# A gated cross-attention block with a routed feed-forward layer: shorter operand stacks, extra TensorE sums, two batches routed together

## The chip, the cores and the metric

One core of one Trainium2 chip runs the whole program. The metric is the device time of one execution in microseconds (us). A tick is the kernel's own unit of order: in one tick each engine handles a fixed list of 16 slots.

## The reference

For 8 batches of 256 tokens with 128 features, and 64 context rows per batch:

```
x = x + tanh(g_xattn) * (attention(layernorm(x), ctx) @ Wout + bout)   # 16 heads of 8; keys: 64 context rows, then the tokens, causal
x = x + tanh(g_ffn) * moe(layernorm(x))
moe:  logits = xt @ Wg + bg; two best of 8 experts per token
      seq = cumsum(one_hot, axis=0)          # a token's place in its expert; over 320 it is dropped
      h = silu(disp @ W1) * (disp @ W2); out = h @ W3      # 320 places per expert, hidden 512
      y = sum over the two experts of softmax weight * out[place]
```

## The kernel before, in words

**First part (0 to 36 us).** Tokens are normalised, turned by TensorE (PE) and multiplied with the query, key and value weights, batch by batch. Queries and keys are needed at fp32 accuracy from bf16 multiplies, so each is split into three bf16 parts (`qp`, `kp`): ScalarE (ACT) writes part 0 and, from a difference that VectorE (DVE) forms (`parts`), part 1; GpSimd (POOL) writes part 2 (`third_parts`). 

**Stacks.** Transfers then pile six pairs of parts on top of one another: for each head of a pair (`par`), `load_q` and `load_k` write six times 8 rows into `qst` and `kst` (48 rows, `QROW`), so that one matmul of 48 rows adds all six products. The stack has 64 rows (`KROWS`): the remaining 16 are -1 in two rows and 0 elsewhere in `kst`, and 0 in `qst`, written by transfers from `fill` and `zeros` (L384, L389). Two of these rows of `qst` are later overwritten with the row maxima (`load_maxima`, L407), so that the second matmul of the scores subtracts the maximum by itself. Batches are loaded in groups of 1, 1, 2, 2, 2. SyncE (SP) issues most transfers, in this order: the parts of group 0, the first halves of group 1, the large fixed-row transfers of groups 1 to 4, a quarter of group 2, then, tick by tick, the maxima of a unit followed by a further quarter of a group. ACT issues the other halves of group 1 (`load_quarter(act, 1, 1)`, `load_quarter(act, 1, 3)`, twelve transfers) before it enters its tick loop, whose first work is the copy of the first unit's maxima (`maxima_row`, L665).

**Units and ticks.** A unit is four head pairs of one batch; there are 16. Unit U is scored in tick U-2 (`scores`: queries on the partitions, only for the maxima, L1037 to L1053), its maxima are reduced by DVE (`maxima`), split and turned (`maxima_t`, L1102) and copied (`maxima_row`) and sent into the stack in tick U-1, it is scored again in tick U with keys on the partitions (`scores_t`, L1070) and exponentiated (`exponentials`, L672), and multiplied with the values in tick U+1 (`values`, L1087), whose result is turned and normalised in tick U+2. A batch is then projected, added to x, normalised, turned, given its logits (`logits`) and routed: `top_two` and `destinations` on DVE, `positions` on PE (places by a triangular matmul, L1165), and four indirect transfers on POOL (`send_rows`, L576). The order on every engine is written out by the constants `AT_...`: a batch's `top_two` begins in tick 3 after its second unit, slot 12; `positions` is in tick 4, slot 13; the rows are sent in tick 5, slots 4, 6, 12 and 20. POOL, DVE, PE and ACT all run their slots in that order, so a wait holds up all that stands behind it on its engine.

**Experts.** When all rows have landed in `slots_dram`, SP loads each expert's 320 rows (`ex`), PE turns them (`turn`, L1207) and runs three matrix multiplies per expert (L1217, L1219, L1230), ACT applies silu, DVE multiplies, and POOL adds the rows to the output with indirect transfers (L607).

PE's code waits, ahead of its first tick, for all constants and for the last difference of the split:

```python
            pe.wait_ge(consts, N_CONSTS)
            pe.wait_ge(cast, 1)
            pe.wait_ge(rq_done, B)
            pe.wait_ge(rk_done, B)
```

## Time and profile before

| | us |
|---|---|
| median of 3 runs (313.08 to 314.41) | 314.01 |
| the profiled execution, its own time | 315.55 |
| its span in the trace | 313.4 |
| PE / DVE / POOL / ACT busy | 220.9 / 174.9 / 153.4 / 131.0 |

"Busy" counts the time an engine has an instruction in work. Rows give start and duration in us from the span's start; `<-` in brackets names what ended an engine's idle time. The granted clock of PE is a share of 2.4 GHz: 1.0 is 2.4 GHz, 0.5 is 1.2 GHz. `ACTq` and `SPq` are the issuing side of those engines, where a transfer is handed to the queue.

### The profile page before, as it was taken

What the parts mean: (1) busy time and instruction counts of PE and PEld (TensorE: products, weight loads), DVE (VectorE), ACT (ScalarE), POOL (GpSimd) and SP (SyncE); (2) the same over time, 40 slices, a digit from 0 to 9 for tenths busy, and PEclk for the clock granted to TensorE, in tenths of its full rate; (3) what the DMA queues carried; (4) which work ended last, traced back from release to release, by engine and by line L of the source; (5) the groups of instructions that cost most, each with busy time, mean ns of one, the idle gap of its engine ahead of it and who ended that gap; (6) DMA issues with size and microseconds to landing.
All of it is one profiled execution on the core that took longest, in us unless ns stands there. A gap on an engine that the chain in (4) does not pass through costs nothing.

```text
span 313.4 us, 6289 instructions
## 1 busy us (share of the span) xinstructions
PE 220.9 (70%) x2308; PEld 138.4 (44%) x2308; DVE 174.9 (56%) x556; ACT 131.0 (42%) x294; POOL 153.4 (49%) x208
## 2 busy tenths in 40 slices
PE   1878360068898777878888878784049999999830
PEld 0656220044554444444444434343027777777630
DVE  6666390047988998989898962434203333333310
ACT  6479400055766656656565665311023222222200
POOL 6698800014445457382736555453700554654662
PEclk9999755556999999999999985755558999999995
DMA  6342799545354333556110010001045345555220
GB/s 193 76 85 57 92 101 131 123 118 103 98 107 67 51 53 69 85 105 204 32 47 11 18 42 12 3 14 35 9 106 134 83 107 113 119 110 119 23 21 5
DMA packets 30237, 24.14 MB, mean 77 GB/s; under 512 B 4041, under 2 KB 27011, under 8 KB 30208
## 3 DMA queue, kind: packets, MB, share of 16 engines
q1 hardware_dynamic: 23104, 18.08, 28.2%
q0 software_dynamic: 4608, 4.16, 7.6%
q10 hardware_dynamic: 2496, 1.52, 1.8%
q8 instruction: 18, 0.29, 0.4%
q14 instruction: 11, 0.09, 0.1%
HBM read 9.27 MB, written 5.82 MB: 48 GB/s over the span
## 4 chain that ended last, share of the span: by engine, by line
PE 48%; DVE 14%; POOL 10%; issue 8%; ACTq 8%; ACT 7%; DMA 2%; POOLq 1%; SPq 0%; DVEq 0%
PE PS L1087 11%; PE PS L1230 8%; PE PS L1217 7%; ACTq L330 6%; PE PS L1219 6%; PE PS L1070 5%; DVE mx L794 3%; ACT pt L672 3%; PE PS L1137 2%; DVE mx L793 2%; POOL slots L576 2%; ACTq L338 2%; POOL rstd L566 2%; PE PS L1154 1%; PE PS L1040 1%
## 5 line engine op out<-in xcount | busy, mean ns | idle before, releaser
L672 ACT ACTIVATE pt<-PS 128x512 f32<-128x512 f32 x128 | 69.3, 593 | 40.9 <-PE PS L1070 40.7
L607 POOL DMA_INDIRECT out<-kst x24 | 36.4, 1518 | 43.9 <-DVE kst L972 31.1
L793 DVE TENSOR_REDUCE mx<-PS 128x2 f32<-128x384 f32 x64 | 35.4, 552 | 34.3 <-PE PS L1053 33.7
L794 DVE TENSOR_REDUCE mx<-PS 128x2 f32<-128x640 f32 x64 | 52.0, 812 | 0.0
L1087 PE MATMUL PS<-pt,vp 128*32 128x256 f32 (+2 forms) x768 | 48.2, 348 | 4.8 <-POOL pt L558 4.8
L1070 PE MATMUL PS<-qst,kst 64*128 64x256 bf16 (+2 forms) x384 | 27.6, 254 | 28.0 <-DMA qst<-mrow 18.2
L555 POOL TENSOR_SCALAR_AFFINE_SELECT pt<-pt 128x512 f32<-128x512 f32 x32 | 21.5, 672 | 52.7 <-ACT pt L672 52.6
L576 POOL DMA_INDIRECT slots<-rows,dest x32 | 32.2, 1005 | 14.6 <-issue 7.6
L963 DVE TENSOR_TENSOR kst<-PS,kst 128x320 f32<-128x320 f32 x32 | 15.7, 491 | 38.5 <-ACT kst L730 38.5
L1070 PEld LDWEIGHTS PS<-qst,kst 64*128 64x128 bf16 x384 | 14.9, 98 | 47.2 <-issue 20.2
L730 ACT ACTIVATE kst<-PS 128x320 f32<-128x320 f32 x32 | 14.0, 438 | 46.7 <-PE PS L1219 46.7
L1217 PE MATMUL PS<-kst,kp 128*128 128x320 f32 x64 | 25.3, 478 | 0.6 <-ACT kst L719 0.6
L1230 PE MATMUL PS<-kp,kst 128*128 128x128 f32 (+1 forms) x192 | 24.3, 279 | 1.3 <-issue 1.1
L1230 PEld LDWEIGHTS PS<-kp,kst 128*128 128x128 f32 (+1 forms) x192 | 21.7, 173 | 6.1 <-issue 5.2
L1087 PEld LDWEIGHTS PS<-pt,vp 128*32 128x32 f32 x768 | 16.1, 115 | 18.1 <-issue 10.0
L1219 PE MATMUL PS<-kst,kp 128*128 128x320 f32 x64 | 23.4, 449 | 0.0
L1040 PE MATMUL PS<-kst,qst 64*128 64x320 bf16 x128 | 21.8, 334 | 0.0
L1037 PE MATMUL PS<-kst,qst 64*128 64x192 bf16 x128 | 17.4, 265 | 5.8 <-POOL blank L527 4.1
L558 POOL TENSOR_SCALAR_AFFINE_SELECT pt<-pt 128x512 f32<-128x512 f32 x32 | 20.2, 633 | 0.0
L1046 PE MATMUL PS<-maskb,halves 64*128 64x256 bf16 x128 | 19.7, 301 | 0.0
L563 POOL TENSOR_SCALAR veps<-mv 128x2 f32<-128x2 f32 x8 | 1.6, 197 | 35.2 <-DVE mv L846 35.2
L972 DVE TENSOR_SCALAR kst<-PS,kst,tgf 128x128 f32<-128x128 f32 (+1 forms) x24 | 8.3, 402 | 18.0 <-PE PS L1230 15.9
(125 smaller groups left out, 365.3 us busy)
## 6 DMA issues: line engine op xcount, KB each, us to landing
kp<-in_w SPq DMA_DIRECT2D x24, 256.0 KB, 2.9
kst<-kp SPq DMA_DIRECT2D x30, 80.0 KB
qst<-qp SPq DMA_DIRECT2D x36, 64.0 KB
slots<-blank POOLq DMA_DIRECT2D x4, 325.0 KB, 4.8
kst<-fill SPq DMA_DIRECT2D x2, 560.0 KB, 12.8
kst<-slots SPq DMA_DIRECT2D x8, 130.0 KB, 2.4
out<-xs SPq DMA_DIRECT2D x4, 256.0 KB, 2.5
qst<-zeros SPq DMA_DIRECT2D x2, 448.0 KB, 15.5
```

The costliest lines, as they stand in the source:

```text
L555: nc.gpsimd.affine_select(out=last, in_=last, compare_op=ALU.is_ge, fill=0.0, base=64, pattern=[[0, UP], [0, 2], [1, 64]], channel_multipl ...
L576: nc.gpsimd.indirect_dma_start(out=slots_dram, out_offset=bass.IndirectOffsetOnAxis(ap=dest[:, b % 2, 2 * t + k:2 * t + k + 1], axis=0), i ...
L607: nc.gpsimd.indirect_dma_start(out=tokens, out_offset=bass.IndirectOffsetOnAxis(ap=ex[0:n, e, s, D:D + 1].bitcast(u32), axis=0), in_=yr[0: ...
L672: nc.scalar.activation(pt[:, U % 2, h, :], PS[:, 4 + h % 2, :], ACT.Exp, scale=SCALE).then_inc(exp_done, 1)
L793: nc.vector.tensor_reduce(mx[:, U % 2, 0, 2 * p:2 * p + 2], PS[:, a:a + 2, 0:192], axis=AX.X, op=ALU.max)
L794: nc.vector.tensor_reduce(mx[:, U % 2, 1, 2 * p:2 * p + 2], PS[:, a:a + 2, 192:512], axis=AX.X, op=ALU.max).then_inc(max_done, 1)
L1040: nc.tensor.matmul(bank[:, 192:512], queries_of(r, gp)[:, g0 + p, i, 128:256], keys_of(r, gp)[:, g0 + p, i, :], start=False, stop=False)
L1070: c = nc.tensor.matmul(PS[:, 4 + par, c0:c1], keys_of(r, gp)[:, g0 + p, i, k0:k0 + 128], queries_of(r, gp)[:, g0 + p, i, q0:N], start=True ...
L1087: c = nc.tensor.matmul(O[VW * j:VW * j + VW, q0:N], vblock(b, chunk, g0 + j, par), pt[:, V % 2, 2 * j + par, c0:c1], start=(chunk == 0 and ...
L1217: nc.tensor.matmul(PS[:, 2 + n % 2, 0:CAP], w1s[:, e % 2, 128 * c:128 * c + 128], xT[:, e % 2, :], start=True, stop=True)
L1219: nc.tensor.matmul(PS[:, 4 + n % 2, 0:CAP], w2s[:, e % 2, 128 * c:128 * c + 128], xT[:, e % 2, :], start=True, stop=True).then_inc(h_ready, 1)
L1230: m = nc.tensor.matmul(PS[0:n, 6 + e % 2, 128 * s:128 * s + D], hid[:, e % 2, c, 128 * s:128 * s + n], w3s[:, e % 2, c, :], start=(c == 0) ...
```

## The change: what it does, and the diff

The stacks have 48 rows in `scores` and 50 rows in `scores_t` (`KROWS = QROW + 2`). The transfers of zeros and of the 16-row fill are gone; `load_minus` writes two rows of -1 per head and group from a `minus` tile, for each group on its own. The wait for them moves from `scores` to `scores_t`. The second part of the keys is written by DVE (`second_part`), no longer by ACT. PE waits for 12 constants ahead of its first tick, no longer for 17.

`keep_active` issues matmuls of `ones` with 512 columns whose result nobody reads: one or two at every fourth slot of the first three ticks and two at every fourth slot of tick 14 and all later ticks (the loop runs to tick 22), and 12, 10 and 12 after the loop, with waits for two small POOL memsets between them, which follow the second and the fourth send of the last batch.

The last two batches (`LATE`) are routed earlier in the order: `top_two`, `positions` and `destinations` follow the logits directly, and the sends follow them. Their positions go to another PSUM bank. Finally ACT applies one silu right after the last batch's exponential.

```diff
-    KROWS = 64
+    KROWS = QROW + 2
...
+        LATE = B - 2
+        LATE_TOP = tuple(3 * SL + 12 + i // 2 for i in range(8))
+        LATE_E01 = 3 * SL + 14
+        LATE_POS = 3 * SL + 15
+        LATE_DEST = (3 * SL + 15, 4 * SL, 4 * SL + 1, 4 * SL + 1, 4 * SL + 2)
+        LATE_SENT = ((4 * SL + 3, 4 * SL + 4, 4 * SL + 20, 4 * SL + 21), (4 * SL + 3, 4 * SL + 4, 4 * SL + 5, 4 * SL + 6))
...
-            sp.wait_ge(consts, 5)
-            sp.wait_ge(zeros_set, 1)
-            for g0, g1 in ((0, 1), (1, len(GROUPS))):
-                b0, b1 = GROUPS[g0][0], sum(GROUPS[g1 - 1])
+            def load_minus(g):
+
+                b0, n = GROUPS[g]
                 for par in range(2):
-
-                    rows_ = slice(64 * par + QROW, 64 * par + KROWS)
-                    fv = fill[:, :]
-                    sp.dma_start(kst[rows_, b0 * PAIRS * KEYS:b1 * PAIRS * KEYS].rearrange("p (a k) -> p a k", k=4 * KEYS),
...
-                    zv = zeros[0:KROWS - QROW, :]
-                    sp.dma_start(qst[rows_, b0 * PAIRS * N:b1 * PAIRS * N].bitcast(fp32)
...
+                    mn = minus[:, :]
+                    sp.dma_start(kst[64 * par + QROW:64 * par + KROWS, b0 * PAIRS * KEYS:(b0 + n) * PAIRS * KEYS]
+                                 .rearrange("p (a k) -> p a k", a=n),
+                                 bass.AP(tensor=mn.tensor, offset=mn.offset,
+                                         ap=[mn.ap[0], [0, n], [1, PAIRS * KEYS]])).then_inc(fixed_in[g], 16)
+
+            sp.wait_ge(consts, 4)
+            load_minus(0)
+            load_part(sp, load_q, QPART, 0, 0, stack_in[0])
+            load_part(sp, load_k, KPART, 0, 0, stack_in[0])
+            load_minus(1)
+            load_part(sp, load_q, QPART, 0, 2, stack_in[0])
+            load_part(sp, load_k, KPART, 0, 2, stack_in[0])
+            load_quarter(sp, 1, 0)
+            load_quarter(sp, 1, 2)
+            load_minus(2)
...
+                    if tick % 4 == 1:
+                        load_minus(3 + (tick - 1) // 4)
...
+                        for late in LATE_SENT:
+                            b = batch_due(tick, slot, AT_SENT[n], late[n])
+                            if b in BATCHES and LATE_SENT[max(b - LATE, 0)] is late:
+                                send_rows(b, n)
+                                if b == B - 1 and n % 2:
+                                    nc.gpsimd.memset(pace[:, n // 2:n // 2 + 1], 0.0).then_inc(halfway, 1)
...
-                act.wait_ge(rk_done, b + 1)
-                nc.scalar.copy(kp[:, 1, b, :], rk[b % 3]).then_inc(k2_done, 1)
...
+                        if b == B - 1:
+
+                            nc.scalar.activation(gate[:, 0, 0:1], tgf[:, :], ACT.Silu)
...
+            def second_part(b):
+                dve.wait_ge(rk_done, b + 1)
+                nc.vector.tensor_copy(kp[:, 1, b, :], rk[b % 3]).then_inc(k2_done, 1)
...
                     norm_tokens(b + 3)
+                second_part(b)
...
-            dve.wait_ge(consts, N_CONSTS)
...
+            def keep_active(bank, n):
+
+                ov = ones[:, :]
+                for _ in range(n):
+                    nc.tensor.matmul(PS[:, bank, :], ones[:, :],
+                                     bass.AP(tensor=ov.tensor, offset=ov.offset, ap=[ov.ap[0], [0, 4], [1, 128]]),
+                                     start=True, stop=True)
...
-                    heads.append((PS[:, a + par, :], slice(64 * par, 64 * par + KROWS), slice(64 * par, 64 * par + 64)))
+                    heads.append((PS[:, a + par, :], slice(64 * par, 64 * par + QROW), slice(64 * par, 64 * par + 64)))
...
+                    pe.wait_ge(fixed_in[gp], 32)
...
-                pe.wait_ge(x1_done, min(b + 2, B))
+                if b < LATE:
+                    pe.wait_ge(x1_done, b + 2)
+                elif b > LATE:
+                    pe.wait_ge(wts_done, S_WTS * (b - 1) + 3)
+                else:
+                    pe.wait_ge(max_done, UP * UNITS)
+                pos = positions_at(b)
...
-            pe.wait_ge(consts, N_CONSTS)
+            pe.wait_ge(consts, 12)
...
+                    if tick <= 0 and slot % 4 == 0:
+
+                        if tick == -2 and slot == 0:
+                            pe.wait_ge(v_done, B)
+                        keep_active(7, 2 if tick == 0 else 1)
+                    if tick >= UNITS - 2 and slot % 4 == 0:
+
+                        if tick == UNITS - 2 and slot == 0:
+                            pe.wait_ge(max_done, UP * UNITS)
+                        keep_active(1, 2)
...
+            keep_active(1, 12)
+            pe.wait_ge(halfway, 1)
+            keep_active(1, 10)
+            pe.wait_ge(halfway, 2)
+            keep_active(1, 12)
```

## Rows read from the trace of the kernel before

**Rows 1.** The page: the span, and the granted clock in 40 equal slices.

```profile
span 313.4 us, 6289 instructions
...
PEclk9999755556999999999999985755558999999995
```

**Rows 2.** Who waited for whom: us in total, times, longest us.

```profile
ACT mrow L665 <- issue: 24.7, 1, 24.7
```

**Rows 3.** Timeline, 34 to 65 us: start, duration, engine, line.

```profile
34.71 19.19 ACTq L330 DMA_DIRECT2D qst<-qp  x5
...
41.78 15.36 SPq L330 DMA_DIRECT2D qst<-qp  x6
...
59.52 0.36 ACT L665 CAST mrow<-PS 16x256 bf16<-16x256 f32 x1 [24.74 <-issue]
...
64.13 0.61 PE L1070 MATMUL PS<-qst,kst 64*128 64x256 bf16 x6 [18.20 <-DMA qst<-mrow]
```

**Rows 4.** The page's transfers: count, KB each, us to landing.

```profile
kst<-fill SPq DMA_DIRECT2D x2, 560.0 KB, 12.8
...
qst<-zeros SPq DMA_DIRECT2D x2, 448.0 KB, 15.5
```

**Rows 5.** Stretches: PE, PEld, DVE, ACT, POOL busy, clock, DMA share, GB/s.

```profile
44.00:46.00 2.00, 1.43 (x14) 0.56 (x10) 2.00 (x4) 0.00 (x0) 0.00 (x0) 0.50 0.95 105
62.00:64.00 2.00, 0.00 (x0) 0.00 (x0) 0.00 (x0) 0.00 (x0) 0.00 (x0) 0.50 0.50 131
```

**Rows 6.** Timeline: end of the first part, first scores, first turned maxima, ACT's transfers.

```profile
33.44 0.46 ACT L644 CAST kp<-work 128x320 bf16<-128x320 f32 x1
...
35.98 0.34 PE L1037 MATMUL PS<-kst,qst 64*128 64x192 bf16 x2 [4.06 <-POOL blank L527]
...
42.37 0.38 PE L1102 MATMUL PS<-identb,mxb 128*16 128x128 bf16 x2 [0.68 <-DVE mxb L806]
...
59.54 4.18 ACTq L338 DMA_DIRECT2D kst<-kp  x6
```

**Rows 7.** Timeline of SP: the maxima of units 2, 3 and 4.

```profile
74.14 1.33 SPq L407 DMA_DIRECT2D qst<-mrow  x2
...
81.89 1.32 SPq L407 DMA_DIRECT2D qst<-mrow  x2
...
88.47 1.33 SPq L407 DMA_DIRECT2D qst<-mrow  x2
```

**Rows 8.** Timeline of PE at the full clock, in the steady part.

```profile
145.79 0.30 PE L1040 MATMUL PS<-kst,qst 64*128 64x320 bf16 x2
145.92 0.27 PE L1046 MATMUL PS<-maskb,halves 64*128 64x256 bf16 x2
146.03 0.22 PE L1053 MATMUL PS<-maskb,halves 64*128 64x128 bf16 x2
146.18 0.43 PE L1087 MATMUL PS<-pt,vp 128*32 128x64 f32 x16
```

**Rows 9.** Timeline: start of tick 14, the last unit's maxima, start of tick 15.

```profile
181.90 0.40 PE L1070 MATMUL PS<-qst,kst 64*128 64x256 bf16 x6 [0.32 <-ACT pt L672]
...
183.81 1.26 SPq L407 DMA_DIRECT2D qst<-mrow  x2
...
192.16 0.61 PE L1070 MATMUL PS<-qst,kst 64*128 64x256 bf16 x6 [0.69 <-ACT pt L672]
```

**Rows 10.** Stretches late in the run, columns as in rows 5.

```profile
185.00:186.00 1.00, 0.88 (x10) 0.28 (x7) 0.50 (x3) 0.05 (x1) 0.23 (x1) 0.86 0.03 8
209.00:220.00 11.00, 4.66 (x22) 3.01 (x22) 4.89 (x33) 1.63 (x6) 3.44 (x6) 0.50 0.10 29
231.00:237.00 6.00, 5.24 (x11) 3.33 (x12) 0.49 (x1) 2.15 (x3) 0.00 (x0) 0.51 0.54 134
```

**Rows 11.** Timeline: the last batch's positions, its last send, the first expert's turn.

```profile
219.93 0.19 PE L1165 MATMUL PS<-lab,tri 128*128 128x8 bf16 x1 [1.59 <-DVE lab L887]
...
226.28 0.98 POOL L576 DMA_INDIRECT slots<-rows,dest  x1 [0.30 <-issue]
...
231.16 0.99 PE L1207 MATMUL PS<-ident,kst 128*128 128x128 f32 x3 [10.94 <-DMA kst<-slots]
```

More of the change, by code:

```diff
@@ L75, in flamingo_gated_block @@
         bb = sb("bb", [128, D])
-        fill = sb("fill", [16, 4 * KEYS], bf16)
+        minus = sb("minus", [2, PAIRS * KEYS], bf16)
         wgs = sb("wgs", [128, E])
@@ L188, in flamingo_gated_block @@
         vp_set = sem("vp_set")
-        fixed_in = [sem(f"fixed_in{i}") for i in range(2)]
+        fixed_in = [sem(f"fixed_in{g}") for g in range(len(GROUPS))]
         consts = sem("consts")
@@ L303, in due, with batch_due @@
             return n // SL if n % SL == 0 else None
-        def batch_due(tick, slot, at):
+        def batch_due(tick, slot, at, late_at=None):
             U = due(tick, slot, at)
-            return U // 2 if U in EVERY and U % 2 else None
+            if U in EVERY and U % 2 and (late_at is None or U // 2 < LATE):
+                return U // 2
+            if late_at is not None:
+                U = due(tick, slot, late_at)
+                if U in EVERY and U % 2 and U // 2 >= LATE:
+                    return U // 2
+            return None
         O = PS[:, 6, 0:N]
@@ L465, in _ @@
             nc.gpsimd.memset(half[:, :], -0.5).then_inc(consts, 1)
-            nc.gpsimd.memset(fill[:, :], 0.0).then_inc(consts, 1)
-            pool.wait_ge(consts, 4)
-            nc.gpsimd.memset(fill[0:2, :], -1.0).then_inc(consts, 1)
+            nc.gpsimd.memset(minus[:, :], -1.0).then_inc(consts, 1)
             def rstd_of(g):
@@ L876, in top_two @@
                 if step == 4:
+                    if b == 0:
+                        dve.wait_ge(consts, N_CONSTS)
                     dve.wait_ge(route, r + 4)
@@ L953, in _ @@
                     for step in range(8):
-                        if (b := batch_due(tick, slot, AT_TOP[step])) in BATCHES:
+                        if (b := batch_due(tick, slot, AT_TOP[step], LATE_TOP[step])) in BATCHES:
                             top_two(b, step)
                     for step in range(5):
-                        if (b := batch_due(tick, slot, AT_DEST[step])) in BATCHES:
+                        if (b := batch_due(tick, slot, AT_DEST[step], LATE_DEST[step])) in BATCHES:
                             destinations(b, step)
@@ L1158, in positions @@
             def positions(b):
+                if b == 0:
+                    pe.wait_ge(consts, N_CONSTS)
                 pe.wait_ge(lab_ready, b + 1)
                 pe.wait_ge(route, S_ROUTE * b)
-                pe.wait_ge(x1_done, min(b + 2, B))
-                cur, rn = lab[:, b % 2, :, :], run[:, b % 2, :]
-                nc.tensor.matmul(POS[:, 0, :], tri[:, :], cur[:, 0, :], start=True, stop=False)
-                nc.tensor.matmul(POS[:, 0, :], ones[:, :], rn, start=False, stop=True)
-                nc.tensor.matmul(POS[:, 1, :], tri[:, :], cur[:, 1, :], start=True, stop=False)
-                nc.tensor.matmul(POS[:, 1, :], ones[:, :], cur[:, 0, :], start=False, stop=False)
-                nc.tensor.matmul(POS[:, 1, :], ones[:, :], rn, start=False, stop=True).then_inc(pos_ready, 1)
-            pe.wait_ge(consts, N_CONSTS)
+                if b < LATE:
[5 more added lines that the diff above has]
+                pos = positions_at(b)
+                cur, rn = lab[:, b % 2, :, :], run[:, b % 2, :]
+                nc.tensor.matmul(pos[:, 0, :], tri[:, :], cur[:, 0, :], start=True, stop=False)
+                nc.tensor.matmul(pos[:, 0, :], ones[:, :], rn, start=False, stop=True)
+                nc.tensor.matmul(pos[:, 1, :], tri[:, :], cur[:, 1, :], start=True, stop=False)
+                nc.tensor.matmul(pos[:, 1, :], ones[:, :], cur[:, 0, :], start=False, stop=False)
+                nc.tensor.matmul(pos[:, 1, :], ones[:, :], rn, start=False, stop=True).then_inc(pos_ready, 1)
+            pe.wait_ge(consts, 12)
             pe.wait_ge(cast, 1)
@@ L1197, in _ @@
                         logits(b)
-                    if (b := batch_due(tick, slot, AT_POS)) in BATCHES:
+                    if (b := batch_due(tick, slot, AT_POS, LATE_POS)) in BATCHES:
                         positions(b)
+            keep_active(1, 12)
[3 more added lines that the diff above has]
+            keep_active(1, 12)
             def turn(e):
```

38 lines of the change are left out of this document (12 added, 26 removed).

## The prediction

> **What bounds the kernel now.** I read the page first: its clock line [rows 1] shows two holes at half clock (0.5, which is 1.2 GHz), slices 5 to 9 (about 39 to 76 us) and 24 to 29 (about 188 to 235 us, with one slice of 0.7). Then the waits: the longest single one is ACT's, 24.7 us ahead of the copy of the first unit's maxima, put down to "issue" [rows 2]. The timeline shows why [rows 3]. ACT hands transfers to its queue from 34.71 us on; five of them take 19.19 us, and only after twelve does it come to L665, at 59.52. SP is stuck beside it (six transfers, 15.36 us). Tick 0 starts at 64.13, and PE idled 18.20 us ahead of it. What clogs the queues is the fixed rows: two transfers of 560 KB and two of 448 KB, 12.8 and 15.5 us to landing [rows 4]. While they move, the DMA engines are 0.95 busy at 105 GB/s; when only stack rows move, 131 GB/s pass at a share of 0.50 [rows 5]. So the first hole is a transfer problem, and its length is a time nobody computes in.
>
> The middle is a steady beat: from the maxima of unit 4 (88.47) to those of unit 15 (183.81) [rows 7, 9] 11 ticks pass in 95.3 us, 8.67 each. The change leaves it alone. Tick 14, without scores, still takes 10.26 us [rows 9], because the clock falls at about 185.9 [rows 10]. The end of that part is one chain: positions of the last batch at 219.93, four sends, loads, first turn at 231.16 [rows 11]. The experts begin at half clock (0.51 over 231 to 237 us, PE busy 5.24 of 6) [rows 10].
>
> **Part A, the ramp.** Removed: 2,016 KB of fixed rows for groups 1 to 4; added: five times two small transfers, 10 KB per head and batch by the diff (160 KB in all). The first scores are at 35.98 now, held by the last POOL constant (the bracket says L527). Afterwards PE waits for the key difference of the last batch, which is there before 33.44 [rows 6]. I take the first part itself as unchanged: ACT loses a cast of 0.46 us per batch [rows 6], and DVE gains one of about the same length; ACT is the fuller engine late in that part and DVE early. Between the ends, 3.7 us less (8 x 0.46) and 3.7 more, I take zero, since both kinds of batches occur. So scores start at 33.5.
>
> First turned maxima come 42.37 + 0.38 - 35.98 = 6.8 us later, at 40.3. ACT's twelve transfers now run freely: six took 4.18 us [rows 6], twelve 8.4 us, from about 33.4 to 41.8. That is later than 40.3, so ACT's issuing still sets the copy at 41.8. From the copy to tick 0 it was 64.13 - 59.52 = 4.6 us [rows 3]. Tick 0 starts at 46.4: **17.7 us less**. Bounds: if the maxima alone set it, 44.9 (19.2 less); if data does, some 816 KB of stack rows (ACT's 432, SP's 384 by the shapes) and 325 KB of clearing of the slots at 105 GB/s take 10.9 us from 33.4, then 4.6: 48.9 (15.2 less). The other stack rows (two further groups' worth over the next ticks) have the same ticks to land in as before. The two `load_minus` of group 1 stand ahead of SP's third parts of group 0 and those of group 3 and 4 behind the maxima; each costs SP some 1.3 us (two issues, like the two of L407 [rows 7]), in which SP otherwise waits for other engines.
>
> **Part B, ticks 0 and 1.** Both ran mostly at half clock. Tick 1 to 2 took 81.89 - 74.14 = 7.75 us, the next 88.47 - 81.89 = 6.58 at full clock [rows 7]. So full clock is worth 1.2 us a tick there. In its favour stand the added sums, 8 in tick 0. Their price: 320 columns go by in 145.92 - 145.79 = 0.13 us at full clock [rows 8], so 512 columns take 0.21 us, and 0.43 at half. While PE waits for the maxima's transfer it issues nothing, so I expect tick 0 to begin at half clock, fill up with sums, and the clock to rise by tick 1: **1.2 less**; the ends are 2.4 less (full from the start) and 1.0 more (sums at half clock in the way).
>
> **Part C, ticks 14 to 18.** The sums put 8 x 0.21 = 1.7 us of PE work per tick where the scores were. The steady tick with scores keeps its clock, so I take it kept. Tick 14 then is no longer than the steady 8.67, and no shorter than 6.58 [rows 7], the nearest tick that carries little; I take 8.3, 2.0 less. Tick 15 was about 9.3 long (an estimate between tick 14 and the steady tick); 8.0 now, 1.3 less. Tick 16 gains by the clock and loses by the new order: `positions` of batch 6 now stands ahead of `turn_values` of the last unit on PE, and `destinations` ahead of its `invert` on DVE. I count zero. The last chain, 209 to 220 us, has 4.66 us of PE work at 0.50 [rows 10]; half of it at best is 2.3, of which fixed latencies keep some: 1.5 less. The earlier routing of batch 6 itself gives little: its sends precede those of batch 7 anyway, and batch 7's chain ends last. The sum of part C is **4.8 less**, between 0 (clock not held) and 6.5.
>
> **Part D, sums ahead of the experts.** After the last `positions` PE still has ticks 19 to 22 (4 x 8 = 32 sums) and 34 behind the loop, 66 x 0.213 = 14.1 us at full clock. Until now 231.16 - 220.1 = 11.1 us passed there [rows 11]. The waits for the memsets are met before PE comes to them, since the last send starts 226.28 - 219.93 = 6.4 us after the positions and the first 44 + 10 sums take 11.5. So the first turn comes at least 3.0 us late, more if some sums run at half clock. I take **3.6 more**, up to 17.2 (all at 0.43). The memsets on POOL are hidden by this.
>
> **Part E, experts.** They begin at full clock. PE's 5.24 us in 231 to 237 at 0.51 [rows 10] would shrink to half, 2.6; I take **2.3 less**. The early silu moves a table load that half-speed matmuls had covered.
>
> Sum: -17.7 - 1.2 - 4.8 + 3.6 - 2.3 = **-22.4 us**. Against the profiled execution's 315.55 us this gives 293.2; its span of 313.4 becomes 291.0. That execution was 1.5 us above the median of 314.01, so the median becomes 291.6.
>
> What does a sum cost beside its columns? In the trace a values matmul (128*32) starts at 146.18, 0.07 us before the scores matmul (64*128) ahead of it ends (146.03 + 0.22) [rows 8]: changing the tile shape costs nothing that shows. The Trainium skill (TensorEngine Tiling (Array Packing), Key Properties) says that changing the tiling mode drains TensorE. The trace does not bear it out here, and the sum above goes by the row; by the page it would be that of the fourth rival.
>
> **The rivals.**
> 1. The queues stay slow. If ACT's twelve transfers stretch half way to what they took (34.7 to 59.5), tick 0 begins near 53 and the ramp gives 11: about 298. For it: both queues feed the same DMA engines and SP now issues a quarter of group 2 in the same time. Against it: 59.54 on, when both also issue, ACT needs 0.70 us each [rows 6]. 0.12.
> 2. The clock holds from the first scores through the last sums: ramp -19.2, B -2.4, C -5.5, D +3.1, E -2.6, together -26.6: 287.4. For it: PE's pause ahead of the scores is shorter. Against it: scores alone left PE idle a quarter of the time (1.43 of 2 us busy, [rows 5]) and never brought the clock back. 0.15.
> 3. The clock falls in ticks 14 to 18 in spite of the sums and comes back late: C 0, D +7.1 (some sums at half speed), so -17.7 - 1.2 + 7.1 - 2.3 = -14.1: 299.9. 0.10.
> 4. Each group of sums drains the array twice: 4 groups x 2 x 0.22 us (the scores matmul's own length [rows 8]) in ticks 14 and 15, where PE has no slack, is 3.5 us less 0.8 for partial cover, 2.7: 294.3. 0.05.
> 5. Slower: the sums do not bring the clock at all. Place: PE at 0.5 from tick 14 to the experts. Ticks 14 and 15 get 16 x 0.43 = 6.8 us of work, of which 5.0 shows, the next ticks 1.5, part D 17.2, tick 0 1.0: 24.7 more, against 17.7 less: 321. It decides once the sums cost over 17.7. Against it: the clock rose after each dense stretch of matmuls so far (at the end of tick 1 and in the experts). 0.03.
>
> **How the numbers follow.** The forecast as summed has 0.55, with 288.5 to 294.5 as its own range. The full range takes in rivals 1, 2 and 4 and half of rival 3: 286 to 299. A measurement here can tell about 0.5% (1.6 us) from no change. Only rival 5 lies above that (0.03), 0.01 for near-cancellation in between, 0.96 for faster.
>
> **What would show it.** Ramp: no transfer of over 100 KB on SP's queue between 31 and 42 us, twelve ACT issues at 0.7 us, L665 first near 42 and L1070 first near 46; wrong if issues take over 1 us. B: tick 0 near 8 us at half clock, tick 1 below 7. C: tick 14 to 15 about 8.3 instead of 10.26, granted clock 1.0 through 14 and 15. D: from the last L1165 to the first turn over 14 us, PE full of sums, while the first expert's rows landed some 3 us before; wrong if the first turn waits for its DMA. E: clock 1.0 at the first up matmul. The steady tick stays at 8.67; if it changes, something I have left out acts. The forecast as a whole is wrong if tick 0 starts after 50 us or if the clock stays at 0.5 in ticks 14 to 18.

## The result and the profile after

| | before | after |
|---|---|---|
| median, us (lowest to highest, runs) | 313.86 (313.08 to 314.41, 4) | 300.88 (298.69 to 302.58, 4) |
| the profiled execution, its own time / its span, us | 315.55 / 313.4 | 302.21 / 300.5 |
| PE / DVE / POOL / ACT busy, us | 220.9 / 174.9 / 153.4 / 131.0 | 239.7 / 176.5 / 154.0 / 127.7 |

The ratio is 0.958 (0.951 to 0.966): 13.0 us less, where 22.4 were forecast. The time lies 1.9 us above the predicted range. Some executions of a kernel ran a few per cent longer at a lower granted clock: the ratios and their intervals here and below leave these out, the medians and ranges hold all.

The page of the changed kernel, its clock line and the group of the sums; these answer to [rows 1]:

```profile
span 300.5 us, 6540 instructions
...
PEclk9989996879997999999999999986999999999995
...
L1054 PE MATMUL PS<-ones 128*128 128x512 bf16 x122 | 34.5, 408 | 0.1
```

Both holes of [rows 1] are nearly gone from the clock line, and yet over 9 us of the forecast gain are missing. To see where they went, I cut both profiled executions at five marks: the start of tick 0, ACT's copies of the maxima of units 3 and 15, the positions of the last batch, and the first turn of the experts.

| stretch, us | before | after | difference | forecast |
|---|---|---|---|---|
| start to tick 0 | 64.13 | 47.27 | -16.9 | -17.7 |
| to the maxima of unit 3 | 17.4 | 20.3 | +3.0 | -1.2 |
| to the maxima of unit 15 | 101.9 | 103.3 | +1.4 | 0 |
| to the last positions | 36.5 | 33.5 | -2.9 | -4.8 |
| to the first turn | 11.2 | 16.0 | +4.7 | +3.6 |
| to the end | 82.3 | 80.1 | -2.2 | -2.3 |
| sum | 313.4 | 300.5 | -12.9 | -22.4 |

**The ramp.** The timeline of the changed kernel, 33 to 51 us, with the rows that answer to [rows 3, 6]:

```profile
33.69 0.26 PE L1071 MATMUL PS<-kst,qst 48*128 48x192 bf16 x2 [1.39 <-DVE work L792]
34.24 3.67 ACTq L351 DMA_DIRECT2D qst<-qp  x5
37.95 4.00 ACTq L359 DMA_DIRECT2D kst<-kp  x6
39.63 0.28 PE L1137 MATMUL PS<-identb,mxb 128*16 128x128 bf16 x2 [0.73 <-DVE mxb L833]
41.98 0.36 ACT L684 CAST mrow<-PS 16x256 bf16<-16x256 f32 x1 [7.73 <-issue]
...
42.37 1.35 SPq L423 DMA_DIRECT2D qst<-mrow  x2
...
47.27 0.61 PE L1105 MATMUL PS<-qst,kst 50*128 50x256 bf16 x6 [4.36 <-DMA qst<-mrow]
```

ACT's eleven transfers after the first take 7.7 us where five alone took 19.2, the copy of the first maxima (L684, which was L665) comes at 41.98 and tick 0 at 47.27. The turned maxima are there at 39.63, so it is ACT's issuing that still sets the copy.

**Ticks 0 and 1.** The same timeline goes on with SP's transfer of the maxima of unit 1 and the first matmul of tick 1:

```profile
48.56 1.04 PE L1054 MATMUL PS<-ones 128*128 128x512 bf16 x2
50.33 1.33 SPq L423 DMA_DIRECT2D qst<-mrow  x2
56.89 0.39 PE L1105 MATMUL PS<-qst,kst 50*128 50x256 bf16 x6 [2.36 <-DMA qst<-mrow]
```

The stretches behind it, columns as in [rows 5]:

```profile
46.00:50.00 4.00, 2.73 (x20) 1.14 (x22) 1.29 (x2) 1.14 (x3) 0.00 (x0) 0.50 0.57 77
50.00:54.00 4.00, 3.71 (x47) 1.96 (x44) 2.58 (x4) 2.83 (x6) 1.26 (x2) 0.90 0.57 77
58.00:62.00 4.00, 3.54 (x36) 1.70 (x38) 2.29 (x4) 1.72 (x4) 1.25 (x2) 0.50 0.49 134
```

The maxima of unit 1, 4 KB a transfer, are issued at 50.33, and PE gets on only at 56.89, 6.6 us later. Meanwhile stack rows move at only 77 GB/s. PE idles 2.36 us for these maxima, and the clock, up again at 50 to 54 us, is back at 0.50 over 58 to 62.

**From tick 14 on.** The last ticks, the routing and the sums, answering to [rows 9, 11]:

```profile
169.33 0.40 PE L1105 MATMUL PS<-qst,kst 50*128 50x256 bf16 x6 [0.31 <-ACT pt L691]
...
178.03 0.40 PE L1105 MATMUL PS<-qst,kst 50*128 50x256 bf16 x6 [0.37 <-ACT pt L691]
...
204.45 0.19 PE L1206 MATMUL PS<-lab,tri 128*128 128x8 bf16 x1 [0.72 <-DVE lab L916]
...
204.60 15.97 PE L1054 MATMUL PS<-ones 128*128 128x512 bf16 x66
210.53 0.98 POOL L593 DMA_INDIRECT slots<-rows,dest  x1 [0.30 <-issue]
...
220.41 0.58 PE L1264 MATMUL PS<-ident,kst 128*128 128x128 f32 x3
```

Tick 14 now takes 8.70 us (it was 10.26). Then 66 sums in a row fill 15.97 us, and PE comes to the first turn without waiting for its rows. In [rows 11] the same turn had waited 10.94 us for them.

### The profile page after: what moved, and what is told of

The parts are those of the page before. It is cut to its first block, busy times and chain, and to the rows that moved or that the text cites. A ratio compares the mean times of both kernels' runs of the same rounds, so it can differ in the third digit from the quotient of the medians.

```text
span 300.5 us, 6540 instructions
## 1 busy us (share of the span) xinstructions
PE 239.7 (80%) x2430; PEld 143.1 (48%) x2430; DVE 176.5 (59%) x564; ACT 127.7 (43%) x287; POOL 154.0 (51%) x209
## 4 chain that ended last, share of the span: by engine, by line
PE 39%; DVE 19%; issue 12%; POOL 11%; DMA 8%; ACT 3%; ACTq 2%; another core or an unknown queue 1%; POOLq 1%; SPq 0%; DVEq 0%
PE PS L1122 9%; PE PS L1054 6%; DMA out<-kst 4%; PE PS L1105 4%; PE PS L1287 4%; PE PS L1274 4%; DVE mx L821 4%; DMA qst<-mrow 3%; POOL out L628 3%; PE PS L1276 3%; DVE mx L820 3%; DVE rows L878 2%; ACT pt L691 2%; PE PS L1172 1%
## 5 line engine op out<-in xcount | busy, mean ns | idle before, releaser
L1122 PE MATMUL PS<-pt,vp 128*32 128x256 f32 (+2 forms) x768 | 46.0, 332 | 3.8 <-POOL pt L575 3.8
L593 POOL DMA_INDIRECT slots<-rows,dest x32 | 32.2, 1005 | 19.5 <-DVE dest L959 12.6
L991 DVE TENSOR_TENSOR kst<-PS,kst 128x320 f32<-128x320 f32 x32 | 15.7, 491 | 41.3 <-ACT kst L752 40.1
L1105 PE MATMUL PS<-qst,kst 50*128 50x256 bf16 (+2 forms) x384 | 26.3, 244 | 15.7 <-DMA qst<-mrow 6.7
L1054 PE MATMUL PS<-ones 128*128 128x512 bf16 x122 | 34.5, 408 | 0.1
L1105 PEld LDWEIGHTS PS<-qst,kst 50*128 50x128 bf16 x384 | 14.5, 96 | 34.5 <-issue 19.4
L1274 PE MATMUL PS<-kst,kp 128*128 128x320 f32 x64 | 24.2, 460 | 0.6 <-ACT kst L741 0.6
L1122 PEld LDWEIGHTS PS<-pt,vp 128*32 128x32 f32 x768 | 15.2, 111 | 19.2 <-issue 11.7
L1276 PE MATMUL PS<-kst,kp 128*128 128x320 f32 x64 | 22.4, 432 | 0.0
L1074 PE MATMUL PS<-kst,qst 48*128 48x320 bf16 x128 | 20.0, 305 | 0.0
L1071 PE MATMUL PS<-kst,qst 48*128 48x192 bf16 x128 | 16.5, 252 | 2.7 <-DVE work L792 1.4
L1080 PE MATMUL PS<-maskb,halves 64*128 64x256 bf16 x128 | 18.3, 280 | 0.0
```

The source lines that it names most:

```text
L593: nc.gpsimd.indirect_dma_start(out=slots_dram, out_offset=bass.IndirectOffsetOnAxis(ap=dest[:, b % 2, 2 * t + k:2 * t + k + 1], axis=0), i ...
L1054: nc.tensor.matmul(PS[:, bank, :], ones[:, :], bass.AP(tensor=ov.tensor, offset=ov.offset, ap=[ov.ap[0], [0, 4], [1, 128]]), start=True, s ...
L1105: c = nc.tensor.matmul(PS[:, 4 + par, c0:c1], keys_of(r, gp)[:, g0 + p, i, k0:k0 + 128], queries_of(r, gp)[:, g0 + p, i, q0:N], start=True ...
L1122: c = nc.tensor.matmul(O[VW * j:VW * j + VW, q0:N], vblock(b, chunk, g0 + j, par), pt[:, V % 2, 2 * j + par, c0:c1], start=(chunk == 0 and ...
L1274: nc.tensor.matmul(PS[:, 2 + n % 2, 0:CAP], w1s[:, e % 2, 128 * c:128 * c + 128], xT[:, e % 2, :], start=True, stop=True)
L1276: nc.tensor.matmul(PS[:, 4 + n % 2, 0:CAP], w2s[:, e % 2, 128 * c:128 * c + 128], xT[:, e % 2, :], start=True, stop=True).then_inc(h_ready, 1)
```

## The experiments

**My theory** was that the transfers bring the whole gain, that the stall in tick 1 is queued transfer work, and that the 66 sums make the experts late. **The rival** was that the clock kept up by the sums is a large part of the gain, and that it is the sums that made the first ticks longer. Three series of kernels were timed, each with the kernel before beside it. All of them, cut as above; medians in us, and the ratio to the kernel before with its interval:

| kernel | median (range) | ratio | tick 0 | to unit 3 | to unit 15 | to positions | to turn | to end |
|---|---|---|---|---|---|---|---|---|
| before, as shown | 313.86 | | 64.1 | 17.4 | 101.9 | 36.5 | 11.2 | 82.3 |
| after, as shown | 300.88 | 0.958 (0.951 to 0.966) | 47.3 | 20.3 | 103.3 | 33.5 | 16.0 | 80.1 |
| the change again | 302.52 (298.16 to 303.97) | 0.947 (0.940 to 0.954) | 47.2 | 19.2 | 103.6 | 33.0 | 17.0 | 80.1 |
| stacks only | 298.77 (296.48 to 301.17) | 0.961 (0.938 to 0.985) | 48.1 | 19.2 | 102.0 | 33.4 | 11.3 | 82.0 |
| no sums | 299.85 (295.59 to 301.29) | 0.960 (0.931 to 0.989) | 47.7 | 19.0 | 103.1 | 34.9 | 11.0 | 82.5 |
| no first sums | 301.41 (300.81 to 304.09) | 0.975 (0.963 to 0.987) | 47.4 | 19.9 | 102.1 | 33.3 | 16.2 | 80.1 |
| trimmed sums | 296.35 (294.80 to 297.38) | 0.957 (0.949 to 0.965) | 47.3 | 19.1 | 102.1 | 33.3 | 11.1 | 80.1 |
| trimmed, no late routing | 296.24 (296.04 to 297.75) | 0.946 (0.942 to 0.949) | 47.9 | 17.7 | 102.8 | 34.0 | 11.8 | 80.1 |
| trimmed, quarter sooner | 295.99 (294.75 to 297.79) | 0.944 (0.940 to 0.948) | 49.0 | 16.4 | 102.9 | 33.7 | 10.8 | 80.1 |
| trimmed, bridge alone | 296.86 (296.24 to 298.83) | 0.948 (0.944 to 0.952) | 48.3 | 19.5 | 103.4 | 33.5 | 10.8 | 80.1 |
| sums at the end only | 299.81 (294.37 to 301.02) | none | 47.3 | 20.4 | 104.6 | 35.9 | 10.9 | 80.1 |
| maxima by ACT | 294.99 (294.46 to 296.66) | 0.936 (0.931 to 0.940) | 48.1 | 16.7 | 103.7 | 33.0 | 11.0 | 80.1 |
| and bridge | 295.82 (293.72 to 299.73) | 0.938 (0.932 to 0.943) | 47.9 | 15.7 | 104.4 | 33.0 | 10.8 | 80.1 |
| and sums in tick 18 | 294.39 (292.24 to 295.20) | 0.932 (0.927 to 0.937) | 47.8 | 15.8 | 104.5 | 33.0 | 10.8 | 80.1 |

The kernel before took 314.71 us in the first series ("stacks only" to "trimmed sums"), 313.58 in the second ("no late routing" to "sums at the end only") and 314.85 in the third ("maxima by ACT" to the last row, with "the change again"). In the first its seven executions were unusually spread, three at 309 to 310 us and four at 315 to 317, so the ratios of this series are wide and don't compare with those of the others. Medians of different series are compared with some 1 us of doubt, and with more where the first series takes part.

### The transfers alone

The edit puts only the stack part of the diff (48 and 50 rows, `load_minus`, no clearing) on the kernel before: no sums, routing and `second_part` as before.

> Only the first part of the change on the kernel before: stacks of 48 and 50 rows, small transfers of -1 in place of the large ones, the wait moved. No added sums, old routing order, the cast of the second key part still on ScalarE, TensorE waits for all constants. If the transfers are nearly the whole gain (theory), tick 0 starts about 16 us earlier than in the kernel before (at 48 us), some 3 to 4 us of that are lost again in ticks 1 to 7, and the time is about 300 to 302 us. If the gain hangs on the added sums as much (rival), it stays above 305 us.

Measured: 298.77 us. The page, then the timeline of PE:

```profile
span 295.9 us, 6293 instructions
...
PEclk9999855589999999999999955965569999999995
```

```profile
57.85 0.61 PE L1066 MATMUL PS<-qst,kst 50*128 50x256 bf16 x6 [3.05 <-DMA qst<-mrow]
...
213.94 0.99 PE L1203 MATMUL PS<-ident,kst 128*128 128x128 f32 x3 [10.96 <-DMA kst<-slots]
```

With both clock holes still in its clock line, this kernel shows no loss against the full change: 298.77 us against 300.88 and 302.52 of other series, and in its own series against 301.41 of the change without its first sums. That is less than the 300 to 302 us expected. Its ramp gain (16.0) arrives in full at the end: the span is 17.5 us shorter. The stall in tick 1 is there too (3.05 us), so it comes with the early start, not with the sums. And the stretch from the maxima of unit 15 to the positions is 33.4 us, no longer than with sums near the full clock. This stretch of the kernel before, of the stacks alone and of the changed kernel, columns as in [rows 5]:

```profile
183.43:219.93 36.50, 25.63 (x233) 12.91 (x233) 13.90 (x83) 12.03 (x30) 18.65 (x26) 0.58 0.08 23
169.25:202.68 33.43, 22.44 (x232) 11.40 (x233) 13.98 (x83) 12.04 (x30) 18.66 (x26) 0.68 0.09 25
170.90:204.45 33.55, 26.68 (x271) 11.66 (x271) 14.60 (x83) 12.53 (x31) 20.29 (x27) 0.95 0.09 26
```

The first two have the same order and no sums, and yet the second is 3.1 us shorter, with PE's clock (the third number from the end) at 0.68 instead of 0.58. So a gain as large as the changed kernel's 2.9 us here stands in a profile without sums and without the new order.

### Without sums, without the first sums

```diff
-                    if tick <= 0 and slot % 4 == 0:
...
-                        keep_active(7, 2 if tick == 0 else 1)
-                    if tick >= UNITS - 2 and slot % 4 == 0:
...
-                        keep_active(1, 2)
...
-            keep_active(1, 12)
-            pe.wait_ge(halfway, 1)
-            keep_active(1, 10)
-            pe.wait_ge(halfway, 2)
-            keep_active(1, 12)
```

The second kernel leaves out only the first of the three blocks.

> The changed kernel without any of the sums nobody reads. Theory: the sums of ticks 14 and 15 brought 2.9 us and the full clock at the experts 2.2, the surplus of sums ahead of the experts cost 4.7, the first ones little: so the time is within 1.5 us of the changed kernel, 299.5 to 302.5, with the clock at 0.5 from tick 14 to the experts. Rival (the sums are worth much): over 304 us.

> The changed kernel without the sums of ticks -2 to 0. Theory: tick 0 begins at half clock with or without them, because TensorE waits there for a transfer; the clock comes back later in ticks 0 to 2; the time changes by less than 1.5 us. Rival: the sums carry the first ticks, and without them mrow of unit 2 is sent 2 us later. Second rival: the sums are in the way there at half clock, and without them it is 1 us earlier.

Measured: 299.85 and 301.41, against 300.88 and 302.52 of the two measurements of the full change, both as expected. All of the sums together are worth nothing that shows. The cuts say why: without any, the experts take 82.5 us and the stretch to the positions 34.9; with them it is 80.1 and 33.0 to 33.5, but from the positions to the first turn 16.0 to 17.0 us instead of 11.0. The first sums alone change the stretch to unit 3 little: 19.9 us without them, 20.3 and 19.2 with them.

### Fewer sums ahead of the experts

```diff
-                    if tick >= UNITS - 2 and slot % 4 == 0:
+                    if UNITS - 2 <= tick <= UNITS + 2 and slot % 4 == 0:
```

> The changed kernel with the sums inside the loop ending at tick 18, so that 34 and not 66 stand between the last positions and the first turn of the experts. Theory: the surplus of sums held up the first turn by 5 us (its rows had landed at about 215.4, it began at 220.4), so this gains 4.5 to 5 us: 296 us. Rival: the clock falls in the pauses for the two small memsets and the experts begin at half clock, which gives 2.2 back: 298 us. Second rival: nothing, since the first turn waits for its rows: 301 us.

Measured: 296.35, as expected. No run is in common with the full change (its slowest run 297.38, the fastest of the change 298.16), but those were timed in other series; in its own it is 5.1 us below the change without its first sums (301.41, lowest 300.81). The timeline of PE:

```profile
202.01 6.85 PE L1054 MATMUL PS<-ones 128*128 128x512 bf16 x22
...
209.10 2.76 PE L1054 MATMUL PS<-ones 128*128 128x512 bf16 x12 [0.24 <-POOL pace L616]
212.93 0.64 PE L1264 MATMUL PS<-ident,kst 128*128 128x128 f32 x3 [1.07 <-DMA kst<-slots]
```

The last 12 sums now wait for the memset after the last send, and the turn waits 1.07 us for its rows: the rows set the turn again, 4.98 us after the last send at 207.95. Counted from its own last send (210.53), the changed kernel's rows were there at about 215.5, an estimate; it turned at 220.41. So the 32 sums of ticks 19 to 22 cost 4.9 us and bring nothing: the experts take 80.1 us either way.

### Sums at the end only

The trimmed kernel's 34 sums after the loop stay, all others go (the first two blocks of the diff above).

> The trimmed kernel with only the 34 sums between the last positions and the experts; none in the first ticks and none in ticks 14 to 18. Theory: the experts still run at full clock from the start (82.3 us from the first turn to the end becomes 80.1), ticks 14 to 18 lose 1 to 3 us depending on when the clock falls: 296.5 to 299. Rival: 34 sums behind a stretch at half clock don't bring the clock up in time, and turn to end is 82 us.

Measured: 299.81, above the 299 expected, and no ratio: the four executions took 294.37, 299.50, 300.12 and 301.02 us, and the profile is of the last. The experts start at full clock (80.1), which shows that the sums after the loop alone are enough for that. Whether the sums of ticks 14 to 18 are worth their place stays open with this run.

### The late routing

On the trimmed kernel:

```diff
-        LATE = B - 2
+        LATE = B
```

> The trimmed kernel with the last two batches routed in the old order (LATE = B). Theory: the earlier routing is worth less than 1 us, since the last batch's chain ends last in both orders and its sends start as soon as its destinations are there; from the last unit's maxima to the last positions it stays 33 to 34.5 us. Rival: with PE faster than before, the four sends of batch 6 (1.28 us each) now stand in the way of those of batch 7 in the old order, and it is 2 to 4 us slower.

Measured: 296.24 against 296.35. The timeline of POOL shows what the order does; here the four sends of the last batch (from 205.22 on) follow the last send of the batch before (203.94) back to back:

```profile
203.94 0.98 POOL L593 DMA_INDIRECT slots<-rows,dest  x1 [0.30 <-DVE dest L959]
205.22 0.98 POOL L593 DMA_INDIRECT slots<-rows,dest  x1 [0.30 <-issue]
206.51 0.98 POOL L593 DMA_INDIRECT slots<-rows,dest  x1 [0.30 <-issue]
...
209.07 0.98 POOL L593 DMA_INDIRECT slots<-rows,dest  x1 [0.30 <-issue]
```

From the positions to the turn it takes 11.8 us instead of 11.1, and the positions come 0.6 us later after the last maxima. The late routing is worth some 1.4 us in one profile of each, and nothing that the medians show.

### The stall in tick 1

The quarter of group 2 that SP issues between the maxima of units 0 and 1, the second of four, is moved ahead of both, on the trimmed kernel:

```diff
             load_quarter(sp, 2, 0)
+            load_quarter(sp, 2, 1)
...
-                if tick < 1:
-                    load_quarter(sp, 2, tick + 2)
-                elif tick < 9:
+                if tick == 0:
+                    load_quarter(sp, 2, 2)
+                elif 1 <= tick < 9:
```

> The trimmed kernel with SyncE's second quarter of group 2 issued ahead of the first maxima (about 37.5 us, when SyncE has nothing to issue) and not behind them. Theory: the transfer of the maxima of unit 1 (50.3 to 56.8 us) waits in its queue behind 864 KB of stack rows that move at 77 GB/s, which holds up tick 1 by 2 us and drops the clock; with the quarter out of the way it lands before 54.5, tick 1 starts without a wait for it, and 2 to 3 us are gained (294 us), less up to 1 us if the first maxima now wait. Rival: the wait only moves to the first maxima, and tick 0 starts 2 us or more later: no gain.

Measured: 295.99, where 294 was expected. The timeline of PE with the starts of ticks 0, 1 and 2:

```profile
49.02 0.61 PE L1106 MATMUL PS<-qst,kst 50*128 50x256 bf16 x6 [5.36 <-DMA qst<-mrow]
...
57.30 0.40 PE L1106 MATMUL PS<-qst,kst 50*128 50x256 bf16 x6 [0.35 <-ACT pt L692]
...
63.98 0.39 PE L1106 MATMUL PS<-qst,kst 50*128 50x256 bf16 x6 [0.68 <-DMA qst<-mrow]
```

Tick 1 does not wait for a transfer any more, which settles what it waited for: the transfer of the maxima behind stack rows of a later group. The DMA records of the two traces show the same directly. In the changed kernel 248 packets (the pieces in which the trace records a transfer) of stack rows, 260 KB, pass on SP's queue between the issue of the maxima of unit 1 at 50.33 and their own first packet at 54.81; here none does (issued 52.08, first packet 53.33). The stretch to unit 3 falls from 19.1 to 16.4 us, below the 17.4 of before. But tick 0 itself starts 1.7 us later, tick 2 now waits 0.68 us for its maxima, and the longer steady part (102.9 against 102.1) takes most of the rest.

A second way was to leave the stall and cover PE's pause before tick 0 with 20 sums, so that the clock would be up:

```diff
                 for slot in range(SL):
+                    if tick == 0 and slot == 0:
+                        keep_active(7, 20)
```

> The trimmed kernel with 20 more sums between the last scores of tick -1 and the first of tick 0, where TensorE waits 4.4 us for the first maxima. Theory: the clock then holds through tick 0, whose sums no longer take twice as long, so the maxima of unit 1 are sent 1 us sooner; but tick 1 waits for their transfer anyway, so the total gains under 1 us. Rival: the clock in the ramp is what costs, and 2 to 3 us are gained.

Measured: 296.86, nothing gained. A stretch of it, columns as in [rows 5]:

```profile
58.00:62.00 4.00, 3.48 (x34) 1.65 (x36) 2.34 (x4) 1.78 (x4) 1.25 (x2) 0.50 0.49 132
```

The stall in tick 1 is still there (2.6 us), and the clock falls behind it as in the changed kernel. A clock brought up ahead of a stall is lost in it. The 20 sums also overran: PE was in them until 48.3, so tick 0 began at 48.33 without a wait, 1.0 us later than in the trimmed kernel.

### All of it together

Three kernels build on the quarter moved: ACT issues the maxima of unit 0 itself, then 16 sums ahead of tick 0, then 8 sums instead of 2 at the start of tick 18. The changed kernel was timed once more in the same series.

```diff
                         maxima_row(U)
                         if U == 0:
+                            act.wait_ge(mrow_done, 1)
+                            for par in range(2):
+                                row = 64 * par + QROW
+                                act.dma_start(queries_of(slice(row, row + 2), 0)[:, 0:UP, 0, :],
+                                              mrow[2 * UP * par:2 * UP * par + 2 * UP, 0, :]).then_inc(m_in[0], 16)
                             load_quarter(act, 2, 3)
```

```diff
+                    if tick == 0 and slot == 0:
+                        keep_active(7, 16)
...
-                        keep_active(1, 2)
+                        keep_active(1, 8 if (tick, slot) == (UNITS + 2, 0) else 2)
```

> The changed kernel once more, beside the three below. Theory: its runs spread over some 4 us, because the granted clock falls in some of them once more in the steady part; the median stays at 299 to 302 us, and the step from the maxima of unit 6 to those of unit 7 is 8.0 us in a profile without such a fall and 9.1 with one.

> Trimmed sums, SyncE's second quarter of group 2 ahead of the first maxima, and the maxima of unit 0 sent by ScalarE's queue, which is nearly empty then. Theory: what held up the two first maxima was the queue that they shared with stack rows, so now neither waits: tick 0 starts at 47 us or earlier (49.0 with SyncE's queue), tick 1 without a wait for a transfer, and the time is 293.5 to 295.5. Rival: the DMA engines themselves are shared by both queues, tick 0 starts at 49 again, and it stays at 296.

> The kernel before this one with 16 sums ahead of tick 0's first scores. Theory: with the stall of tick 1 gone the bridged clock now holds through ticks 0 to 2, and 1 to 2 us are gained over the run without the bridge. Rival: the clock falls by its own in tick 1 or 2, no gain.

> The kernel before this one with 8 in place of 2 sums at the start of tick 18, where TensorE waits some 2.6 us for the last batch's norm and the clock fell at 199 to 201 us in the other runs. Theory: the clock holds there, the last turn and logits take 0.4 us less, and the total changes by under 1 us. Rival: the 8 sums reach past the norm and delay the turn by up to 1 us.

Measured: 302.52 (0.5 above what was expected), 294.99, 295.82 and 294.39. The first timeline is of the kernel with ACT's maxima alone:

```profile
43.20 1.34 ACTq L727 DMA_DIRECT2D qst<-mrow  x2
...
48.13 0.61 PE L1111 MATMUL PS<-qst,kst 50*128 50x256 bf16 x6 [5.08 <-DMA qst<-mrow]
```

The 1.7 us by which the moved quarter made tick 0 late are two things: ACT's copy of the maxima came 0.7 us later (42.68, it was 42.01), and from the copy to tick 0 it took 6.3 us instead of 5.3. Handing the transfer to ACT's queue takes the second away (5.3 us again, from 42.81) and leaves the first. It is still 4.9 us from issue to tick 0, and tick 0 misses the 47 us expected: ACT's queue was not nearly empty. By the DMA records 235 packets (172 KB) of ACT's own stack rows pass on it before the first packet of the maxima, at 46.59. In the changed kernel, also 4.9 us from issue to tick 0, no stack row stands ahead of the maxima on SP's queue; there their packets run from 43.91 to 45.44, and PE starts 1.8 us after the last. The page and PE's timeline of the last kernel:

```profile
PEclk9999959989999989999999999999999999999995
```

```profile
43.10 0.22 PE L1093 MATMUL PS<-maskb,halves 64*128 64x128 bf16 x2
43.24 3.84 PE L1060 MATMUL PS<-ones 128*128 128x512 bf16 x17
47.78 0.39 PE L1111 MATMUL PS<-qst,kst 50*128 50x256 bf16 x6 [0.69 <-DMA qst<-mrow]
...
54.67 0.40 PE L1111 MATMUL PS<-qst,kst 50*128 50x256 bf16 x6 [0.35 <-ACT pt L692]
...
61.96 0.40 PE L1111 MATMUL PS<-qst,kst 50*128 50x256 bf16 x6 [1.28 <-DMA qst<-mrow]
...
211.90 0.64 PE L1272 MATMUL PS<-ident,kst 128*128 128x128 f32 x3 [0.79 <-DMA kst<-slots]
```

With the stall in tick 1 gone the bridge does its work: tick 0 runs at the full clock (a first matmul of 0.39 us instead of 0.61) and takes 6.9 us. The stretch to unit 3 is 15.8 us, 4.5 below the changed kernel's. Part of the stall has only moved: tick 2 waits 1.28 us for its maxima, and the clock is at 0.60 over 62 to 66 us. The steady part gives 1.2 of the 4.5 back. The last kernel has the lowest median of all, 294.39, and a ratio of 0.932 (0.927 to 0.937), where the changed kernel of the same series has 0.947 (0.940 to 0.954): some 5 us (8.1 by the medians of all executions). Among the last three the medians lie within 1.4 us, and their ranges overlap; which of the two groups of sums helps is not shown, and the 1 to 2 us expected of the bridge did not come in the medians. The 8 sums in tick 18 do hold the clock (1.00 over 196 to 201 us, 0.82 without them), and the stretch to the positions stays at 33.0 us.

## Why the prediction was wrong where it was

**Part A, the ramp: right.** Scores 33.69 (33.5 said), ACT's issues done at 41.95 (41.8), the copy 41.98, tick 0 47.27 (46.4). Most of the 0.8 us missing lies in copy to tick 0, 5.3 us instead of the 4.6 taken from before. Rival 1 is out; by its own words (half way between 8.4 and 24.8 us) it would have been tick 0 near 54.6 and not 53.

**The step that failed: "The other stack rows (two further groups' worth over the next ticks) have the same ticks to land in as before."** They had the same ticks, but no longer the same time. Before, much of the queued work had passed while PE stood still for 18.20 us [rows 3]; now tick 0 starts while it is in flight, and the 4 KB of maxima of unit 1 wait behind it. This stall (1.3 to 3.1 us of waiting) stands in every profile with the shorter stacks and the old order of quarters; in tick 1 it goes when the quarter is moved, and 0.7 to 1.4 us of it come back in tick 2. The stretch to unit 3 is 3.0 us longer where 1.2 less were forecast (4.2 us of the 9.5 missed). Moving the quarter gave 2.7 us of this stretch back, so the stall and the clock lost behind it are the larger part; the same code took 1.1 to 1.2 us less there in two other profiles.

**Part B** named the right prices: a tick at full clock 1.2 us shorter, sums at half clock up to 1.0 us in the way. From the copy for unit 0 to that for unit 1 it was 7.97 us instead of 6.31 before: 0.7 from copy to tick 0, and 1.0 from tick 0 to the next copy (2.7 us; 1.7 before, and 1.7 without the first sums). So the bound of 1.0 more is what came, since the clock rose only after 50 us, and it fell again behind the stall. The kernel with the stall in tick 1 gone and the bridge has what was forecast: 15.8 us to unit 3, 1.6 less than before.

**"The middle is a steady beat ... The change leaves it alone"** failed by 1.4 us. The steps from copy to copy are the same to 0.1 us in all the kernels, but for one (unit 9 to 10, 9.43 to 10.10) and for those in which the clock falls. The maxima of unit 6 to 7 took 9.07 us in the changed kernel's profile and 8.09 in the other profile of the same kernel, which instead took 10.62 from unit 13 to 14, where 9.42 is usual. Two stretches of the first profile, then three of the second, columns as in [rows 5]:

```profile
86.00:91.70 5.70, 4.30 (x78) 2.78 (x80) 5.06 (x18) 3.46 (x9) 1.95 (x3) 1.00 0.47 72
92.00:94.00 2.00, 2.00 (x18) 0.65 (x18) 1.99 (x8) 0.88 (x3) 1.10 (x2) 0.50 0.04 12
```

```profile
85.00:90.60 5.60, 4.20 (x78) 2.73 (x72) 5.00 (x18) 3.36 (x9) 1.95 (x3) 1.00 0.47 70
92.00:94.00 2.00, 2.00 (x32) 0.95 (x32) 2.00 (x6) 1.06 (x3) 1.01 (x2) 1.00 0.12 36
154.00:157.00 3.00, 3.00 (x28) 1.31 (x32) 1.09 (x3) 1.57 (x4) 2.69 (x4) 0.50 0.07 23
```

The first line of each is the same piece of work, with PE busy three quarters of it in both; the clock fell behind it at 91.7 in the one and stayed up in the other. Each such fall costs 1.0 to 1.2 us, and where it comes differs from one execution to the next. The shown profile of before has none in this part, and that of the stacks only has none either. Why one execution has a fall and another none stays open.

**Part C: half right.** The clock is held as forecast: 1.00 from 170 to 200 us, and tick 14 takes 8.70 (8.3 said). Of 4.8 us 2.9 came. (The clock fell at 185.7 before, not at 185.9, which changes nothing.) The last chain, forecast 1.5 less, gained nothing: the clock was lost again at about 201 us, where PE had waited for the last batch. The stretch and POOL's timeline of the changed kernel:

```profile
200.00:210.00 10.00, 8.48 (x33) 3.75 (x34) 3.27 (x23) 2.37 (x5) 5.01 (x7) 0.66 0.02 4
```

```profile
198.05 0.98 POOL L593 DMA_INDIRECT slots<-rows,dest  x1 [0.30 <-issue]
199.10 0.19 POOL L580 TENSOR_SCALAR veps<-mv 128x2 f32<-128x2 f32 x1
```

POOL takes up the norm of the last batch (L580) only behind the third send of the batch before: 0.9 us after its statistics, the input, were there at 198.20 (197.90 and 0.30 us by DVE's timeline). That is a small wait that the new order put on the chain. And the reason I gave for part C is not borne out. The kernel with stacks only came through the same stretch in 33.4 us with no sums at a mean clock of 0.68, that without sums but with late routing in 34.9. What the sums and their clock give in this stretch depends on the order: 1.4 to 1.9 us in the new one (34.9 against 33.0 to 33.5), nothing in the old one (33.4 against 34.0), and the new order's share can't be told apart from it. Holding the clock in the last chain too, by the 8 sums of tick 18, left the stretch at 33.0 us: nothing of the 1.5 forecast showed.

**Part D: right in kind, 1.1 short.** "66 x 0.213 = 14.1 us" was 15.97, since the clock was at half for the first 3 us or so of them (0.66 over 200 to 210 us); the turn came 4.7 us later than before (3.6 said; the bound of 17.2 is 17.3 by its own terms), and its rows lay ready for an estimated 4.9 us. The forecast saw this loss, and the trimmed kernel confirms it by giving it back.

**Part E: right.** The experts take 80.1 us instead of 82.3, 2.2 less (2.3 said).

Of the rivals, the second needed the clock to hold from the first scores on, which neither profile of the change shows. The third and the fifth fell, as the clock held from tick 14 on; that the measured 300.88 lies near the third's 299.9 is chance. The fourth, draining between tile shapes, was dismissed by a wrong reading of [rows 8]. The profile models the ends of matmuls, and those of one shape overlap by more: 256 columns end 0.16 us after the next start (145.92 + 0.27 against 146.03), at the change of shape it is 0.07. The starts are the better measure. Of one shape, 320 columns take 0.13 us to the next start and 256 take 0.11; at the change 128 columns take 0.15 (146.03 to 146.18), where 0.05 would be in proportion. In the last kernel above it is 0.14 from such scores at 43.10 to the sums at 43.24, while one sum follows another of its shape after 0.22 (512 columns). So a change of shape costs about 0.1 us here, which bears out what the Trainium skill (TensorEngine Tiling (Array Packing), Key Properties) says of a drain when the mode changes. The sum had put this at nothing and the fourth rival at 0.22: four groups of sums a tick with at most two added changes each come to at most 0.8 us a tick, an estimate from these starts. No run tests what part of that is covered by waits.

By terms of the two profiled executions (22.4 less forecast, 12.9 come), 9.5 us were missed: A 0.8, ticks 0 to 2 4.2, the steady part 1.4, C 1.9, D 1.1, E 0.1.

## What to carry to other kernels

When a start-up stall is taken away, the work that had been hidden in it moves into the first steps behind it: look at each transfer that was in flight during the stall, and at which small and urgent one now stands behind it. Idle-time work for the clock has to end before the next real work is ready, or it becomes the bound; here 32 sums too many gave back more than twice what the higher clock brought, and a wait for the event that comes just before (the last send) placed the rest rightly. And run each part alone: the transfers alone gave all that the whole change gave (298.77 us against 300.88 and 302.52).

## What the runs showed of the hardware that was not expected

- The rate of small stack rows depends on the moment: 77 GB/s at a share of 0.57 over 46 to 54 us of the changed kernel, 134 GB/s at 0.49 over 58 to 62, and 131 at 0.50 in [rows 5]. In the first, both queues hold many transfers; what holds the engines up there was not found.
- Two transfers of 4 KB took 4.9 to 6.6 us from issue to the matmul behind them while stack rows were in flight. Behind 260 KB of these on their own queue, SP's, it was 6.6 us (50.33 to 56.89), behind 172 KB on ACT's queue 4.9 (43.20 to 48.13), and also 4.9 with none ahead on their queue (42.37 to 47.27).
- A change of PE's tile shape (64*128 to 128*32, 64*128 to 128*128) costs about 0.1 us from start to start: 128 columns take 0.15 and 0.14 us where 0.05 would be in proportion (146.03 to 146.18 before, 43.10 to 43.24 in the last kernel).
- The same work can keep the clock or lose it: behind a stretch with PE busy 4.30 of 5.70 us the clock fell at 91.7 in one profile of the changed kernel, and behind the same work, 4.20 of 5.60, it stayed up in the other. At 1.0 to 1.2 us a fall, this can be part of why the executions of its first measurement differ by 3.9 us (298.69 to 302.58).
